# Sorting the edges of a graph layer on the chip into tile pairs, in place of fetching a row for each edge

## Chip, cores and metric

The kernel runs on 1 core of one Trainium2 chip. The metric is device microseconds for one execution. A core has TensorE (PE, matmuls), VectorE (DVE), ScalarE (ACT), GpSimd (POOL) and SyncE (SP), each of which executes its own instructions in program order and waits on semaphores for the others.

## The reference, cut to what matters

A small graph transformer of two layers over 625 nodes with 256 channels and 20000 edges (`src`, `dst`). The change lies in the first graph layer:

```
xl = (x @ W_l).reshape(625, 4, 64)
xr = (x @ W_r).reshape(625, 4, 64)
e = xl[src] + xr[dst]                      # 20000 x 256
e = where(e >= 0, e, 0.2 * e)
score = einsum('ehd,hd->eh', e, att)       # 20000 x 4
# softmax over the edges of each dst, then the weighted sum of xl[src] per dst
```

Beside it stand a token mixer on the same nodes (layer norm, a small attention, an MLP of 1024 hidden channels), then a mixture of 16 experts, then a second layer of the same kinds. Neither kernel differs in these.

## The kernel before

The softmax is done densely. Four scores for each edge are written to a table in HBM with a cell for each (dst, src) pair, of 625 x 625 cells, and a count of how often each pair occurs (`cnt`) is kept in SBUF; attention then runs over dense rows, with the logarithm of the count added. So the edge stage has two products, the scores in `pair_scores` and the counts in `cnt`, and it ends when the last score has landed: SP then loads the tables (L2282), and nothing of the rest can start before.

An edge column is 125 edges, one to a partition; there are 160 columns, in 32 groups of G = 5. For each group:

- GpSimd gathers the xl rows of a column with an indirect DMA (L2143) and scatters the four scores of an earlier column with another (L2153). There are two score tables, taken in turn, and a scatter waits until the one before it on the same table has landed. From group LATE = 12 on, two of five columns get their xl rows from TensorE instead and are not gathered.
- ScalarE makes the one-hot columns that select rows (`hot_rows`, L1888 and L1892).
- TensorE sums rows by multiplying the one-hots with all five node tiles, each in a high and a low part (`rows_of`, L544), and counts the pairs by multiplying two one-hot matrices (`count`, L522).
- VectorE adds gathered and computed rows (L1035, L1125), applies the leaky step (L1013), weighs by `att` (L1018), sums each head (L1021), and makes the one-hots of the counting (L1070, L1071).

The token mixer's steps are written in between the first groups by hand (L477 and L506 up to the MLP, L558 and L566). All groups from 16 to 31 stand in hardware loops.

## Time and profile before

| | |
|---|---|
| three runs | 1161.45, 1166.17, 1166.57 us (median 1166.17) |
| profiled execution, first to last instruction (span) | 1154.3 us |
| busy: PE, DVE, ACT, POOL | 948.9, 858.0, 466.5, 463.7 us |
| last scatter of the edge stage lands | 518.4 us |
| indirect DMAs in the edge stage | 160 scatters, 120 gathers |

The time of a run is the span and some 7 to 12 us around it. Differences are taken within the span and then set against the median. The stages follow each other: edges and mixer up to 518 us, dense attention, experts from about 620 us, the second layer, experts again to the end.

### The profile page before, as it was taken

To read this page: it belongs to the slowest core of one execution; us is meant where nothing else is said; L and a number is where in the kernel's file an instruction comes from. 1 tells how busy PE (TensorE), PEld (TensorE's weight loads), DVE (VectorE), ACT (ScalarE), POOL (GpSimd) and SP (SyncE) were. 2 spreads that over 40 slices of the span, in tenths; PEclk is the share of its full clock that TensorE was granted. 3 is DMA by queue.
4 is the path that set the end of the run, shared out by engine and by line. 5 is a ranking of instruction groups with operands and counts; after the bars stand their busy time and mean duration, and the time that the engine had idled before them with its cause. 6 is when DMAs were issued, how large, how long until landed. Compare 5 with 4: busy or idle time off the path is not lost.

```text
span 1154.3 us, 19240 instructions
## 1 busy us (share of the span) xinstructions
PE 948.9 (82%) x6532; PEld 829.5 (72%) x6532; DVE 858.0 (74%) x1953; ACT 466.5 (40%) x795; POOL 463.7 (40%) x374
## 2 busy tenths in 40 slices
PE   4586998879989998983835999985898588599996
PEld 2566886768978887853734999974588377589885
DVE  5659468869777978997987888776688765866635
ACT  1453755467858686616621111110253053212120
POOL 2448888877777877860001222250000000211104
PEclk9888999789999999997865999997999698699999
DMA  8962222323222232209704999983000000588883
GB/s 295 276 194 64 56 69 68 74 48 73 63 62 62 63 77 47 48 11 247 189 1 137 324 316 333 316 299 116 0 1 1 1 1 1 211 307 304 297 317 91
DMA packets 57946, 157.58 MB, mean 137 GB/s; under 512 B 23797, under 2 KB 32938, under 8 KB 49618
## 3 DMA queue, kind: packets, MB, share of 16 engines
q1 hardware_dynamic: 26830, 125.59, 33.3%
q0 software_dynamic: 25056, 24.10, 9.3%
q10 hardware_dynamic: 5992, 7.04, 1.7%
q8 instruction: 37, 0.61, 0.2%
q14 instruction: 31, 0.25, 0.1%
HBM read 136.50 MB, written 19.86 MB: 135 GB/s over the span
## 4 chain that ended last, share of the span: by engine, by line
PE 33%; DMA 24%; DVE 17%; POOL 12%; issue 10%; SPq 3%; POOLq 0%; ACT 0%; DVEq 0%; ACTq 0%
DMA pair_scores<-sc_ring,idx_ring 13%; PE bank L775 11%; PE bank L786 6%; POOL pair_scores L2153 5%; POOL arena L2143 5%; DMA arena<-pair_scores 4%; PE bank L544 3%; PE bank L708 2%; POOL arena L2208 2%; PE bank L496 2%; SPq L2232 2%; DMA arena<-slot_y,sloti 2%; DMA arena<-in_exp 1%; PE bank L697 1%; PE bank L874 1%
## 5 line engine op out<-in xcount | busy, mean ns | idle before, releaser
L2198 POOL DMA_INDIRECT arena<-row_tab,ids x42 | 57.7, 1373 | 493.7 <-DVE ids L1563 486.6
L2153 POOL DMA_INDIRECT pair_scores<-sc_ring,idx_ring x160 | 210.2, 1314 | 60.3 <-issue 43.4
L2143 POOL DMA_INDIRECT arena<-xl_tab,idx_ring x120 | 157.6, 1313 | 81.3 <-issue 31.7
L775 PE MATMUL bank<-arena 128*128 128x128 f32 x1480 | 180.8, 280 | 3.2 <-DMA arena<-in_exp 3.0
L775 PEld LDWEIGHTS bank<-arena 128*128 128x128 f32 x1480 | 175.0, 197 | 5.3 <-DMA arena<-in_exp 4.1
L1888 ACT ACTIVATE arena<-fmaps,node_neg 125x875 f32<-125x875 int32 x100 | 100.1, 1022 | 34.5 <-PE bank L544 34.5
L786 PE MATMUL bank<-arena 128*128 128x256 f32 (+1 forms) x404 | 97.6, 384 | 1.2 <-DMA arena<-in_exp0o 1.2
L1892 ACT ACTIVATE late_ohT<-arena 125x875 fp32r<-125x875 f32 x100 | 90.6, 926 | 0.0
L2021 ACT ACTIVATE arena<-bank 128x512 f32<-128x512 f32 (+2 forms) x76 | 34.4, 453 | 126.6 <-PE bank L775 126.5
L544 PE MATMUL bank<-late_hi,late_ohT 125*125 125x256 f32 x500 | 83.7, 298 | 0.6 <-DVE arena L1035 0.6
L786 PEld LDWEIGHTS bank<-arena 128*128 128x128 f32 (+1 forms) x404 | 72.1, 190 | 14.9 <-issue 6.0
L522 PE MATMUL bank<-tab 125*128 125x314 bf16 x400 | 62.3, 307 | 17.8 <-DVE tab L1071 17.8
L544 PE MATMUL bank<-late_lo,late_ohT 125*125 125x256 f32 x500 | 76.4, 283 | 0.0
L522 PE MATMUL bank<-tde 125*128 125x314 bf16 x400 | 62.0, 306 | 13.1 <-DVE tde L1071 13.0
L544 PEld LDWEIGHTS bank<-late_hi,late_ohT 125*125 125x125 f32 x500 | 68.8, 191 | 3.3 <-issue 0.9
L544 PEld LDWEIGHTS bank<-late_lo,late_ohT 125*125 125x125 f32 x500 | 67.2, 189 | 0.0
L1950 ACT ACTIVATE arena<-arena,rneg 125x625 f32<-125x625 f32 (+4 forms) x60 | 44.9, 748 | 52.5 <-DVE rneg L1361 26.9
L697 PE MATMUL bank<-ident,arena 125*125 125x125 f32 x260 | 44.1, 302 | 26.5 <-ACT arena L1950 25.5
L544 PE MATMUL bank<-late_hi,early_ohT 125*125 125x256 f32 x300 | 53.0, 312 | 15.4 <-DVE arena L1035 7.7
L1576 DVE TENSOR_TENSOR arena<-bank,arena 128x512 f32<-128x512 f32 (+2 forms) x76 | 37.2, 508 | 35.9 <-ACT arena L2021 35.9
L2000 ACT ACTIVATE arena<-bank 128x256 f32<-128x256 f32 x42 | 16.1, 383 | 116.1 <-DVE arena L1607 81.2
L522 PEld LDWEIGHTS bank<-tab 125*128 125x128 bf16 x400 | 37.2, 100 | 34.5 <-DVE tab L1071 14.9
(357 smaller groups left out, 2017.4 us busy)
## 6 DMA issues: line engine op xcount, KB each, us to landing
arena<-in_exp SPq DMA_DIRECT2D x25, 1024.0 KB, 7.1
arena<-in_exp SPq DMA_DIRECT2D x17, 1386.0 KB, 6.1
arena<-in_exp0o SPq DMA_DIRECT2D x25, 512.0 KB, 7.3
pair_scores<-cnt SPq DMA_DIRECT2D x10, 1093.8 KB
arena<-in_exp1o SPq DMA_DIRECT2D x17, 640.0 KB
fmaps<-in_rows SPq DMA_DIRECT2D x20, 437.5 KB, 3.8
arena<-pair_scores SPq DMA_DIRECT2D x7, 1093.8 KB
slot_y<-arena ACTq DMA_DIRECT2D x34, 128.0 KB, 6.4
```

Source lines behind the costliest of these rows:

```text
L522: mm = pe.matmul(banks[m][:, 0:CW], oh_dst[s][:, j, m * P:m * P + 128], oh_src[s][:, j, :], start=start and j == 0, stop=True, skip_group_ ...
L544: mm = pe.matmul(banks[T + r][0:P, i * D:(i + 1) * D], hot[late, s][:, t, at * P:(at + 1) * P], part[:, t, :], start=(n == 0 and t == 0), ...
L697: mm = pe.transpose(bank[0:P, t * P - off:t * P - off + P], prob[:, i % 3, t * P:(t + 1) * P], ident[0:P, 0:P])
L775: mm = pe.matmul(banks[1 + 2 * q + buf][0:rows, i * SLOTS:(i + 1) * SLOTS], w_in(s, q, k, m, rows), xsT[:, s, k, :], start=(k == 0), stop= ...
L786: mm = pe.matmul(banks[5 + s][:, 0:D], hid[0:rows, s, m, :], w_out(s, m), start=(m == 0), stop=(m == len(flat) - 1))
L1576: ins = v.tensor_tensor(hid[0:rows, s, m0:m0 + n, :], banks[(3 if rows == 128 else 1) + buf][0:rows, i0 * SLOTS:(i0 + n) * SLOTS] .rearran ...
L1888: a.activation(apart[late, s][:, t, :], edge_row[late, s][0:P, :], ACT.Abs, bias=node_neg[:, t:t + 1]).then_inc(sem("apart"), 1)
L1892: ins = a.activation(hot[late, s][:, t - 1, :], apart[late, s][:, t - 1, :], ACT.Relu, scale=-1.0, bias=1.0)
L1950: a.activation(prob[:, i % 3, 0:w], masked[:, i % 3, 0:w], ACT.Exp, bias=rneg[:, i:i + 1], scale=-1.0, accum_out=rden[:, i:i + 1]).then_in ...
L2143: p.indirect_dma_start(out=gat[:, b % 2, 0, j * D:(j + 1) * D], out_offset=None, in_=xl_tab, in_offset=bass.IndirectOffsetOnAxis(ap=idx_ri ...
L2153: p.indirect_dma_start(out=pair_scores[which], in_=sc_ring[:, b % 2, j, :], in_offset=None, out_offset=bass.IndirectOffsetOnAxis(ap=idx_ri ...
L2198: p.indirect_dma_start(out=xs[:, q, :], out_offset=None, in_=tab, in_offset=bass.IndirectOffsetOnAxis(ap=ids[:, q, :], axis=0))\
```

## The change

The edges are first sorted on the chip. A node tile is 125 nodes, so a (dst tile, src tile) pair is one of 25 buckets. VectorE marks the bucket of every edge (`find_buckets`), TensorE counts and ranks the edges in each, and every edge is given a slot, so that each column of 125 slots holds edges of one bucket only, with the rest of the bucket's last column empty. There are SORTED = 184 columns for the 160 of before. The sort itself is a product of one-hot matrices (`sort_edges`): for each of the 160 columns VectorE makes two 125x125 matrices (`choose_places`), GpSimd (three of four) or ScalarE (one of four) a 125x184 one (`find_column`, `find_columns`), and TensorE multiplies them.

Then the 184 columns go in 92 pairs. For a column one tile of xr and one of xl are enough: TensorE transposes two 125x125 one-hots, multiplies them for the counts (`turn_hots`), and sums rows with four matmuls whose second operand stands at an address taken from a register (`sum_rows`). ScalarE copies the one-hots and takes 0.4|z| of the rows (`copy_hots`, `read_rows`), the other part of the leaky step, 0.6z weighed by `att`, comes as four more channels of the tables (ROW = 260). VectorE makes the one-hots, adds the counts at a register address, weighs and sums (`make_hots`, `add_counts`, `score`). GpSimd only scatters; empty slots go to 125 spare cells. No xl table, no gather and no loads of edge rows are left. The mixer's steps stand at fixed pair numbers (`MIX`). All is written out, without loops.

```diff
+BUCKETS = T * T
+SORTED = (E + BUCKETS * (P - 1)) // P
+PAIRS = SORTED // 2
+assert SORTED % 2 == 0
 ROUNDER = 1.5 * 2 ** 23
+TAKEN = 3
+CHOSEN = 6
+HOTS = 3
+SCORED = 16
+MIX_BANKS = 3
...
+MIX = {"ln1": 6, "mixh": 8, "turned": 10, "xm": 11, "qkv_in": 12, "softened": 14, "turned_kq": 15, "kv": 17, "qkv": 18,
+       "attn": 20, "ln2": 22, "h2": 23, "h2T": 25, "m1": 26, "m2": 35, "added": 40}
...
+            def slots():
+                for i, b in enumerate(range(0, BUCKETS, 3)):
+                    after(pe, sem("slots_read"), i - 1)
+                    for q in range(b, min(b + 3, BUCKETS)):
+                        to = banks[3 + i % 2][0:P, (q - b) * EC:(q - b + 1) * EC]
+                        pe.matmul(to, before[:, :], member[:, q, :], start=True, stop=False)
+                        mm = pe.matmul(to, orders[:, q * P:(q + 1) * P], slots_before, start=False, stop=True)
+                    mm.then_inc(sem("slots"), 1)
...
+            def sort_edges():
+                for j in range(EC):
+                    pe.wait_ge(sem("chosen"), j + 1)
+                    if j % 4 == 3:
+                        pe.wait_ge(sem("act_columns"), j // 4 + 1)
+                    else:
+                        pe.wait_ge(sem("pool_columns"), j // 4 * 3 + j % 4 + 1)
+                    for w in range(2):
+                        mm = pe.matmul(banks[5 + w][0:P, 0:SORTED], chosen[:, j % CHOSEN, w, :],
+                                       columns16[:, j % CHOSEN, :], start=(j == 0), stop=(j == EC - 1))
+                    mm.then_inc(sem("placed"), 1)
...
+            def turn_hots(c):
+                pe.wait_ge(sem("onehot"), c + 1)
+                after(pe, sem("counted"), c - 1)
+                bank = banks[4 + c % 2]
+                to_d, to_s = (onehot[:, c // 2 % TAKEN, c % 2, w, :] for w in range(2))
+                pe.matmul(bank[0:P, 0:P], to_d, ident16[:, :], start=True, stop=True)
+                pe.matmul(bank[0:P, P:2 * P], to_s, ident16[:, :], start=True, stop=True)
+                pe.matmul(bank[0:P, 2 * P:3 * P], to_d, to_s, start=True, stop=True).then_inc(sem("turned_hots"), 1)
+            def sum_rows(i):
+                _, rows = nc.values_load_multi_w_load_instructions(
+                    at_rows[0:1, 2 * i:2 * i + 2, :].rearrange("p c w -> p (c w)"), engines=[mybir.EngineType.PE],
+                    min_val=0, max_val=(2 * T - 1) * ROW)
+                for c in range(2):
+                    pe.wait_ge(sem("hot"), 2 * i + c + 1)
+                    after(pe, sem("z_read"), 2 * i + c - 2)
+                    n = 0
+                    for w in range(2):
+                        for part in (hi_rows, lo_rows):
+                            mm = pe.matmul(banks[SUM_BANKS[(2 * i + c) % 3]][0:P, 0:ROW], hot[0:P, i % HOTS, c, w, :],
+                                           part[:, bass.ds(rows[2 * c + w], ROW)], start=(n == 0), stop=(n == 3))
+                            n += 1
+                    mm.then_inc(sem("z_made"), 1)
...
-            def late_group(g, b, segment):
-                s = b % 2
-                for r in range(NP):
-                    rows_of(g, s, 1, r)
-                    if r == 0:
-                        pe.wait_ge(sem("onehot"), g + (1 - BEHIND))
-                        if b == 0:
-                            pe.wait_ge(sem("counts_read"), segment)
-                    mm = count(s, COUNTED[r], b == 0)
...
+            sum_members()
+            pe.wait_ge(sem("ident"), 2)
+            sum_columns()
+            begin_blocks()
+            owners()
+            ring["n"] = 3
+            pe.wait_ge(sem("xn"), T)
+            to_fm("xnT0", xn)
+            slots()
+            pe.wait_ge(sem("wlr_in"), 16)
+            read_out(pe, "xnT0")
+            linear_tm("lr", fa, lambda k: W("lr", k), 2 * D)
+            sort_edges()
+            read_out(pe, "lr")
...
+            turn_hots(0)
+            turn_hots(1)
+            for i in range(PAIRS):
+                for c in (2 * i + 2, 2 * i + 3):
+                    if c < SORTED:
+                        turn_hots(c)
+                sum_rows(i)
+                mix(i)
...
+            def find_buckets():
+                dve.wait_ge(sem("edges_in"), 32 * len(PARTS))
+                own.link(v.tensor_copy(nodes_f, edge_ids[:, :, :]))
+                own.link(v.tensor_scalar(digits, nodes_f, float(P), None, ALU.is_ge))
+                for k in range(2, T):
+                    own.link(v.scalar_tensor_tensor(digits, nodes_f, float(k * P), digits, ALU.is_ge, ALU.add))
+                own.note(v.scalar_tensor_tensor(local, digits, -float(P), nodes_f, ALU.mult, ALU.add))
+                own.link(v.scalar_tensor_tensor(bucket, digits[:, 1, :], float(T), digits[:, 0, :], ALU.mult, ALU.add))
+                for b in range(BUCKETS):
+                    ins = v.tensor_scalar(member[:, b, :], bucket, float(b), None, ALU.is_equal)
+                ins.then_inc(sem("sorting"), 1)
+                own.link(v.tensor_scalar(local, local, 1.0, None, ALU.add))
...
+            def find_slots():
+                for i, b in enumerate(range(0, BUCKETS, 3)):
+                    n = min(3, BUCKETS - b)
+                    dve.wait_ge(sem("slots"), i + 1)
+                    v.tensor_tensor(slot_parts[:, b:b + n, :],
+                                    banks[3 + i % 2][0:P, 0:n * EC].rearrange("p (b j) -> p b j", b=n),
+                                    member[:, b:b + n, :], ALU.mult).then_inc(sem("slots_read"), 1)
+                dve.wait_ge(sem("slots_read"), (BUCKETS + 2) // 3)
+                own.link(v.tensor_reduce(slot_of, slot_parts.rearrange("p b j -> p j b"), AX.X, ALU.add))
+                rounded_of(column_of, slot_of, 1.0 / P, -float(P // 2) / P)
+                own.note(v.tensor_scalar(column_neg, column_of, -1.0, None, ALU.mult))
+                own.link(v.scalar_tensor_tensor(place_of, column_of, -float(P), slot_of, ALU.mult, ALU.add))
+                dve.sem_inc(sem("sorting"), 1)
...
+            def choose_places():
+                for j in range(EC):
+                    after(dve, sem("placed"), j - CHOSEN + 1)
                     for w in range(2):
+                        ins = v.tensor_scalar(chosen[:, j % CHOSEN, w, :], iota_c[:, 0:P], place_of[:, j:j + 1],
+                                              local[:, 1 - w, j:j + 1], ALU.is_equal, ALU.mult)
+                    ins.then_inc(sem("chosen"), 1)
...
+            def make_hots(i):
+                after(dve, sem("turned_hots"), 2 * (i - TAKEN + 1))
+                for c in range(2):
+                    for w in range(2):
+                        ins = v.tensor_scalar(onehot[:, i % TAKEN, c, w, :], iota_1[:, :],
+                                              node_at[:, w, 2 * i + c:2 * i + c + 1], None, ALU.is_equal)
+                    ins.then_inc(sem("onehot"), 1)
+            def add_counts(i):
+                if i == 0:
+                    dve.wait_ge(sem("cnt_zero"), 1)
+                if i % 4 == 0:
+                    n = min(8, SORTED - 2 * i)
+                    _, regs = nc.values_load_multi_w_load_instructions(
+                        at_counts[0:1, 2 * i:2 * i + n], engines=[mybir.EngineType.DVE], min_val=0, max_val=T * N - P)
+                    count_at[:] = regs
+                for c in (2 * i, 2 * i + 1):
+                    dve.wait_ge(sem("hot"), c + 1)
+                    after(dve, sem("counted"), c)
+                    to = cnt_flat[:, bass.ds(count_at[c % 8], P)]
+                    v.tensor_tensor(to, to, banks[4 + c % 2][0:P, 2 * P:3 * P], ALU.add).then_inc(sem("counted"), 1)
...
+            def score(i):
+                rows = weighed[:, i % 2, :, :, :]
+                dve.wait_ge(sem("z_read"), 2 * i + 2)
+                for c in range(2):
+                    ins = v.tensor_tensor(rows[:, c, :, 0:HD], rows[:, c, :, 0:HD],
+                                          Vt(0, "att").rearrange("p (h d) -> p h d", h=H), ALU.mult)
+                    own.note(ins)
...
+                    after(dve, sem(f"scattered{w}"), 16 * (i - SCORED + 1))
+                own.fence()
+                v.tensor_reduce(sc_ring[:, i % SCORED, :, :].rearrange("p c h -> p (c h)"),
+                                rows.rearrange("p c h d -> p (c h) d"), AX.X, ALU.add).then_inc(sem("scored"), 1)
...
+            split_rows()
+            read_nodes()
+            make_hots(0)
+            make_hots(1)
+            find_cells()
+            add_counts(0)
+            for i in range(PAIRS):
+                if i + 2 < PAIRS:
+                    make_hots(i + 2)
+                if i + 1 < PAIRS:
+                    add_counts(i + 1)
+                score(i)
+                mix(i)
+            dve.wait_ge(sem("counted"), SORTED)
...
-            def hot_rows(g, s, late):
-                act.wait_ge(sem(f"rows{s}"), g * 8 + (16 - 8 * s))
-                after(act, sem("z_made"), g * NP - NP)
-                for t in range(T + 1):
-                    if t < T:
-                        a.activation(apart[late, s][:, t, :], edge_row[late, s][0:P, :], ACT.Abs,
-                                     bias=node_neg[:, t:t + 1]).then_inc(sem("apart"), 1)
-                    if t > 0:
-                        act.wait_ge(sem("apart"), g * T + t)
-                        ins = a.activation(hot[late, s][:, t - 1, :], apart[late, s][:, t - 1, :], ACT.Relu,
...
+            def copy_hots(c):
+                act.wait_ge(sem("turned_hots"), c + 1)
+                after(act, sem("z_made"), 2 * (c // 2 - HOTS + 1))
+                a.activation(hot[0:P, c // 2 % HOTS, c % 2, :, :].rearrange("p w n -> p (w n)"),
+                             banks[4 + c % 2][0:P, 0:2 * P], ACT.Copy).then_inc(sem("hot"), 1)
+            def read_rows(i):
+                rows = weighed[:, i % 2, :, :, :]
+                after(act, sem("scored"), i - 1)
+                for c in range(2):
+                    act.wait_ge(sem("z_made"), 2 * i + c + 1)
+                    bank = banks[SUM_BANKS[(2 * i + c) % 3]]
+                    a.activation(rows[:, c, :, 0:HD], bank[0:P, 0:D].rearrange("p (h d) -> p h d", h=H), ACT.Abs, scale=0.4)
+                    a.activation(rows[:, c, :, HD], bank[0:P, D:ROW], ACT.Copy).then_inc(sem("z_read"), 1)
...
+            def find_column(j):
+                after(pool, sem("placed"), j - CHOSEN + 1)
+                p.tensor_scalar(columns16[:, j % CHOSEN, :], iota_c[:, :], column_of[:, j:j + 1], None, ALU.is_equal)\
+                    .then_inc(sem("pool_columns"), 1)
...
+            def scatter(c):
+                which, i = c % 2, c // 2
+                pool.wait_ge(sem("scored"), i + 1)
+                after(pool, sem(f"scattered{which}"), 16 * i)
                 p.indirect_dma_start(
+                    out=pair_scores[which], in_=sc_ring[:, i % SCORED, which, :], in_offset=None,
+                    out_offset=bass.IndirectOffsetOnAxis(ap=pair_cells[:, c:c + 1], axis=0))\```

What the engines execute in the stage, by the compiled programs. First TensorE, a stretch in the middle of a late group of before: `tab` is a counting one-hot, `late_ohT` the row-selecting one-hots, the rest are parts of the tables.

```order
L522 MATMUL bank<-tab 128x314 x10
L544 MATMUL bank<-late_hi,late_ohT 125x256 x5
L544 MATMUL bank<-late_lo,late_ohT 125x256 x5
L544 MATMUL bank<-late_xl_hi,late_ohT 125x256 x5
L544 MATMUL bank<-late_xl_lo,late_ohT 125x256 x5
```

And TensorE in the changed kernel, from the second column's one-hots of a pair to its first two row sums:

```order
L570 MATMUL bank<-ident,mask_words 125x125
L571 MATMUL bank<-ident,mask_words 125x125
L572 MATMUL bank<-mask_words 125x125
L576 TENSOR_LOAD at_rows
L576 ISA x8
L585 ISA
L585 MATMUL bank<-x_hi,hot 125x260
L585 REGISTER_ALU
L585 MATMUL bank<-x_lo,hot 125x260
```

Long runs of equal matmuls have become short ones, with a register load and its moves between them in every pair and a register instruction before each row sum.

VectorE, a stretch of a late group of before (`tde` is a counting one-hot, `tc` the rows to be scored):

```order
L1136 TENSOR_SCALAR arena<-bank 125x512
L1070 ISA
L1070 TENSOR_SCALAR tde<-iota_n,dstf 125x628
L1071 ISA
L1071 TENSOR_SCALAR tde<-iota_n,srcf,src_step 125x314
L165 ISA
L1139 TENSOR_TENSOR tc<-arena,bank 125x512
```

VectorE in the changed kernel, all of one pair (`mask_words` holds the one-hots, `tc` the rows):

```order
L1111 TENSOR_SCALAR mask_words<-iota,node_at 125x125 x4
L1128 ISA
L1128 TENSOR_TENSOR cnt<-cnt,bank 125x125
L1128 ISA
L1128 TENSOR_TENSOR cnt<-cnt,bank 125x125
L1137 TENSOR_TENSOR tc<-tc,vec 125x4x64 x2
L1143 TENSOR_REDUCE sc_ring<-tc 125x8
```

Nine instructions on 125 to 520 elements a partition take the place of ones on 256 to 1280; every fourth pair a load of eight registers comes before the counts.

GpSimd, from the end of its constants into the stage, before:

```order
L2132 IOTA iota_b 125x25
L2136 MEMSET block 32x32 x4
L2143 DMA arena<-xl_tab,idx_ring 125x256 x11
L2153 DMA pair_scores<-sc_ring,idx_ring 390625x4
L2143 DMA arena<-xl_tab,idx_ring 125x256
```

and in the changed kernel, through the stage to the experts' first gathers:

```order
L2106 MEMSET block 32x32 x4
L2113 TENSOR_SCALAR fmaps<-iota_c,tab 125x184 x120
L2132 MEMSET cnt 125x3125
L2120 DMA pair_scores<-sc_ring,pair_cells 390750x4 x184
L2145 DMA arena<-row_tab,ids 128x256 x4
```

The gathers are gone, 120 column operations stand ahead of the first scatter, and 184 scatters follow each other with nothing between.

## Rows read from the trace of the kernel before

**Rows 1.** Windows: length, busy of PE, PEld, DVE, ACT, POOL, clock, DMA share, GB/s.

```profile
400.00:450.00 50.00, 45.58 (x358) 41.07 (x358) 38.59 (x66) 36.38 (x41) 39.13 (x31) 0.97 0.27 66
500.00:520.00 20.00, 14.74 (x97) 9.55 (x96) 19.79 (x45) 4.76 (x7) 11.25 (x10) 0.91 0.09 7
```

**Rows 2.** Groups of GpSimd: x count | busy us, mean ns | idle before.

```profile
L2153 POOL DMA_INDIRECT pair_scores<-sc_ring,idx_ring x160 | 210.2, 1314 | 60.3 <-issue 43.4 <-DMA pair_scores<-sc_ring,idx_ring 16.9
```

**Rows 3.** Timeline of GpSimd, last scatters: start, us, what [idle before].

```profile
508.81 1.19 POOL L2153 DMA_INDIRECT pair_scores<-sc_ring,idx_ring  x1 [1.60 <-DMA pair_scores<-sc_ring,idx_ring]
510.31 1.24 POOL L2153 DMA_INDIRECT pair_scores<-sc_ring,idx_ring  x1 [0.30 <-issue]
512.31 1.25 POOL L2153 DMA_INDIRECT pair_scores<-sc_ring,idx_ring  x1 [0.77 <-issue]
```

**Rows 4.** The chain of waits at the stage's end: start, us, what.

```profile
515.86 2.54 DMA pair_scores<-sc_ring,idx_ring
...
520.16 11.73 DMA arena<-pair_scores
```

**Rows 5.** Timeline of VectorE at the start: first layer norm, from first to last.

```profile
5.71 1.73 DVE L966 BATCH_NORM_STATS2 stats<-x 125x6 f32<-125x256 f32 x5 [1.28 <-DMA x<-in_x]
...
10.38 1.70 DVE L973 TENSOR_SCALAR xn<-x,mv,rstd 125x256 f32<-125x256 f32 x5
```

**Rows 6.** Timeline of TensorE: first linear layer, and a linear layer of the mixer.

```profile
15.18 10.84 PE L496 MATMUL bank<-wres,fmaps 128*125 128x512 f32 x20 [0.64 <-DVE fmaps L989]
...
88.01 5.99 PE L496 MATMUL bank<-wres,fmaps 128*125 128x256 f32 x20 [2.81 <-DVE fmaps L1249]
```

**Rows 7.** Timeline of VectorE: small copies out of PSUM, back to back.

```profile
59.38 0.18 DVE L1204 COPY tde<-bank 125x32 f32<-125x32 f32 x1
59.47 0.41 DVE L1205 COPY tde<-bank 125x256 f32<-125x256 f32 x1
59.80 0.18 DVE L1204 COPY tde<-bank 125x32 f32<-125x32 f32 x1
```

**Rows 8.** Timeline of VectorE: one-hots, back to back, one and two pointer scalars.

```profile
164.40 0.38 DVE L1070 TENSOR_SCALAR tab<-iota_n,dstf 125x628 bf16<-125x628 f16 x1
164.70 0.36 DVE L1071 TENSOR_SCALAR tab<-iota_n,srcf,src_step 125x314 bf16<-125x314 f16 x1
164.97 0.62 DVE L1070 TENSOR_SCALAR tab<-iota_n,dstf 125x628 bf16<-125x628 f16 x1
```

**Rows 9.** Groups of VectorE by shape: the head sums.

```profile
L1021 DVE TENSOR_REDUCE sc_ring<-tc 125x20 f32<-125x1280 f32 x32 | 47.6, 1486 | 3.2 <-DVE tc L1018 1.4 <-DMA pair_scores<-sc_ring,idx_ring 1.1
```

**Rows 10.** Timeline of TensorE: row sums, five to a line, at either clock.

```profile
34.91 1.27 PE L544 MATMUL bank<-late_lo,early_ohT 125*125 125x256 f32 x5
35.98 1.27 PE L544 MATMUL bank<-late_hi,early_ohT 125*125 125x256 f32 x5
...
98.55 0.76 PE L544 MATMUL bank<-late_hi,early_ohT 125*125 125x256 f32 x5
99.14 0.76 PE L544 MATMUL bank<-late_lo,early_ohT 125*125 125x256 f32 x5
```

**Rows 11.** Timeline of SyncE: two issues with one register load between them.

```profile
632.80 0.34 SPq L2318 DMA_DIRECT2D arena<-in_exp  x1
633.90 0.34 SPq L2309 DMA_DIRECT2D arena<-in_exp0o  x1
```

**Rows 12.** Groups of TensorE by shape: the mixer's MLP, up to 640 us.

```profile
L566 PE MATMUL bank<-arena 128*125 128x256 f32 x80 | 17.8, 379 | 0.0
L558 PE MATMUL bank<-fmaps,wres 128*128 128x375 f32 x32 | 11.5, 480 | 2.4 <-DVE fmaps L989 2.4
L558 PE MATMUL bank<-fmaps,wres 128*128 128x250 f32 x32 | 8.0, 374 | 0.0
```

**Rows 13.** Timeline of TensorE: two more pieces of the mixer.

```profile
44.57 4.45 PE L506 MATMUL bank<-fmaps,wres 128*128 128x375 f32 x16 [0.95 <-DVE fmaps L989]
...
59.09 4.38 PE L589 MATMUL bank<-fmaps,mixk 128*32 128x375 f32 x8 [6.50 <-DVE tde L1205]
```

**Rows 14.** Windows again, short ones, for the granted clock (before the DMA share).

```profile
235.00:240.00 5.00, 2.16 (x19) 1.95 (x17) 4.83 (x6) 5.00 (x9) 4.09 (x4) 1.00 0.15 30
600.00:605.00 5.00, 0.55 (x3) 0.55 (x4) 4.52 (x24) 0.00 (x0) 0.00 (x0) 0.50 0.00 0
```

1015 lines of the change are left out of this document (410 added, 605 removed).

## The prediction, made before the result was known

> **What bounds the kernel now.** I read the windows first, then the groups of GpSimd, then the chain. In the middle of the edge stage no engine is idle for long [rows 1]: of 50 us TensorE is busy for 45.6, VectorE for 38.6, ScalarE for 36.4, GpSimd for 39.1. At the stage's end VectorE is (19.8 of 20). So there is no single wait that the change could remove. The reader should see that GpSimd has 160 scatters at 1.31 us each [rows 2], that two scatters on different tables are issued 1.5 us apart (510.31 after 508.81), and on one table 3.5 us apart (512.31 after 508.81) [rows 3], since the second must wait for a landing of 2.54 us. The chain says what the stage's end is worth [rows 4]: the last scatter is issued at 515.86 and lands at 518.40, then the tables are loaded (11.73 us from 520.16), and all that follows waits for that. After this point both kernels do the same. So the question is one number: when does the last of 184 scatters land, against 518.4. Every microsecond there is one in the time. The profiled span is 1154.3, some 12 us under the median of 1166.2; I add the difference to the median. The three runs lie 5 us apart, so under 0.5% (6 us) is no change.
>
> **Up to the first column.** Before the first scatter everything must now be sorted. The edges are there at about 5 us (x lands at 5.7 [rows 5]); the buckets are 25 one-hots of 160 elements and some ten operations on 160 to 320, 7 us, to 12. Then four hand-overs between VectorE and TensorE, each of some small operations and a semaphore either way: I take 3 us each (bounds 1.5 and 4.5), to 24. The layer norm, which now stands behind them, took 5.71 to 12.08, 6.4 us [rows 5], to 30. Transposes and slots: 50 matmuls of 160 columns, with nine products of 480 elements behind them, 14 us (10.5 to 19), to 44. The slots are summed by a reduction of 4000 elements and some more small operations, 7 us, to 51. TensorE's first linear layer took 10.84 us [rows 6] and stands before the sort's matmuls, to 62. Only six columns of one-hots (CHOSEN) can be made ahead of it.
>
> **The sort** runs at VectorE's pace. A small operation costs its elements and a fixed part: a copy of 32 elements takes 0.09 us from start to start, one of 256 takes 0.33 [rows 7], so 1.07 ns an element and 0.06 fixed. A one-hot of 628 elements with one pointer scalar takes 0.30 and one of 314 with two takes 0.27 [rows 8]; a quarter of the time per element fits both, with some 0.065 for each pointer. For 125 elements with two pointers that gives 0.22 at that rate and 0.32 at the copy's; I take 0.27, since the 314-element row has the very same form. Two of them and a wait are 0.57 us a column; 154 columns are 88 us, with a tail 90, to 152 (133 with the low ends throughout, 170 with the high ones). GpSimd has 2.3 us for its three 184-element columns out of four. No row shows such an operation; bounds are nothing (hidden under VectorE) and one indirect issue, 1.19 us [rows 3], which would make 0.89 us a column and 50 us more. I take it as hidden. Splitting the tables into high and low parts is three passes over 2560 elements at the copy's rate, 8.4 us, to 161.
>
> [...]
>
> **A pair of columns.** GpSimd: with one scatter per table and pair, the wait for the same table sets 3.5 us by [rows 3] and issue alone 3.0; I take 3.4. VectorE: four one-hots of one pointer, 0.8; two adds of counts at a register address, 125 elements out of PSUM, 0.3 each; two weighings of 256, 0.33 each and a little; a reduction of 520, by 1486 ns for 1280 [rows 9] 0.63; a share of the register load, 0.3: together 3.2. ScalarE: 1.4. TensorE: eight row sums and six matmuls of 125 columns. Five row sums on 256 columns took 1.07 us from start to start (34.91 to 35.98) and 0.59 (98.55 to 99.14) [rows 10], at the two clocks, so 0.118 or 0.214 each; with a register load of up to 0.76 us (632.80 to 633.90 less the issue, SyncE's, the only one to be seen) [rows 11] and register instructions, 2.4 or 3.7 us. So at full clock GpSimd, VectorE and TensorE stand at 3.4, 3.2 and 2.4: no engine is much ahead, and 92 pairs at 3.4 would be 313.
>
> **The mixer lies on top.** Its MLP takes TensorE 37.3 us [rows 12], its other parts some 27 (4.5 for the MLP-like product of 44.57 [rows 13], 6.0 for the attention's last [rows 6]), VectorE some 40. It stands at pairs 6 to 40 only. Pairs 0 to 5 and 41 to 91 are 57 at 3.4, 194 us. In pairs 6 to 25 VectorE has 20 times 3.2, 34 of the mixer, and waits for TensorE's pieces that stand behind row sums in program order: before, such a wait was 6.50 us ahead of the piece at 59.09 [rows 13]; I take 20 in all: 118. Queued behind each of them are the next pair's one-hots, for which TensorE and then GpSimd wait; a ring of 16 pairs of scores doesn't help, since GpSimd is never that far behind. Pairs 26 to 40: TensorE has 15 times 2.6 and 37 of the MLP, 76. With 5 for filling and the last landing the loop is 393.
>
> **Sum.** 161 + 393 = 554 against 518.4 [rows 4]: 35 us more. 1166 + 35 = 1201. What is removed (120 gathers, the five-tile row sums, the counting over 314 and 628 elements) needs no term of its own, since the stage is summed anew.
>
> **The rivals.**
> *Not paid back* (the forecast, 0.45): some 160 us of preparation, then 393. Its own range, from the bounds of the sort (−20, +18) and of the loop (−8, +15), is 1175 to 1230.
> *Small operations are cheap* (0.30), the other side. If a one-hot is 0.22 and the hand-overs 1.5 us each, blocks begin at 143 or before; if scatters then come every 3.2 us and half of the mixer's 77 us goes into VectorE's and TensorE's gaps, the loop is 294 + 55 + 5 = 354, and the stage ends at 490 to 505: 1138 to 1153. For it: the low ends are rows too, and no engine is full in a pair. Against it: VectorE is full in the mixer's pairs by my sum. It decides when the last scatter is issued before 510; with blocks from 143 that needs under 4.0 us per pair on average. [...]
> *TensorE at half clock* (0.16). [...] At half clock a pair is 3.7 us and the mixer 1.6 times as long: a loop of 450, the stage's end at 611 less what overlaps, some 605: 1250 to 1260. [...]
> *Register loads are dear* (0.09). If the load in every pair stops TensorE, or every fourth pair VectorE, for 1.5 us and more in place of 0.76 and 1.2, that is 0.3 to 0.7 us a pair, 30 to 60 in all: 1235.
>
> **How the numbers follow.** The likeliest case gives 1201. The range 1140 to 1265 runs from the low end of the cheap case to just past the half clock: outside lie the case below 1140 (0.05) and combinations of the dear ones with slow GpSimd columns (0.08). Faster by over 0.5%: 0.27, the cheap case less 0.03 that ends within 6 us of no change. Within: that and 0.04 of the forecast's case, 0.07. Slower: 0.41 + 0.16 + 0.09 = 0.66.
>
> **What would show it.** In the profile of the changed kernel: the first scatter at about 168 us, the one-hots of the sort 0.27 us apart in VectorE's timeline and each column 0.57; the windows from 350 on with a scatter every 1.7 us, both GpSimd and VectorE over 0.8 busy, and the granted clock near 1.00; in pairs 6 to 25 idle times of VectorE before the mixer's operations, with TensorE as releaser; the last landing near 554. Wrong at once: a first scatter before 145, or pairs that come at 3.0 us or under, for which two tables can't be what limits them; or above 4 us after the mixer has ended, which would point at TensorE's clock or the register loads.

## The result, and the profile after

The changed kernel takes 1264.74 us (median of four runs, 1261.63 to 1269.24), the kernel before 1164.11 on the same chip: 1.088 times as long, 95% interval 1.084 to 1.092. So it is 100.6 us slower, where I had forecast 35.

The profiled execution spans 1264.0 us, and its own time was 1265.78. In all runs on record the time is 1.7 to 2.1 us over the span. So the 7 to 12 us that I had put around the span of the kernel before are no fixed part: its profiled execution, at 1154.3, was one of its faster ones. The two profiles are 109.7 us apart for the 100.6 of the medians. The chain of waits shows where the edge stage ends; its columns are start, us, what.

```profile
611.46 2.99 DMA pair_scores<-sc_ring,pair_cells
...
615.31 2.75 DMA pair_scores<-sc_ring,pair_cells
...
618.92 3.26 DMA pair_scores<-sc_ring,pair_cells
...
623.46 12.67 DMA arena<-pair_scores
```

The last scatter lands at 618.92 + 3.26 = 622.2 us, against 518.4 [rows 4]: 104 us later, and I had said 554. What follows took 641.8 us, against 635.9. Before the first scatter, VectorE's timeline is this (start, us, what, in brackets the idle time before and who ended it):

```profile
24.11 1.71 DVE L985 BATCH_NORM_STATS2 stats<-x 125x6 f32<-125x256 f32 x5
...
36.22 0.66 DVE L1071 TENSOR_TENSOR arena<-bank,tde 125x480 f32<-125x480 f32 x1 [5.76 <-PE bank L548]
39.59 0.66 DVE L1071 TENSOR_TENSOR arena<-bank,tde 125x480 f32<-125x480 f32 x1 [2.71 <-PE bank L548]
...
61.74 6.84 DVE L1075 TENSOR_REDUCE tab<-arena 125x160 f32<-125x4000 f32 x1
...
82.47 85.82 DVE L1086 TENSOR_SCALAR mask_words<-iota_c,tab 125x125 bf16<-125x125 f16 x308 [8.15 <-PE bank L560]
```

The hand-overs end at 24 and the layer norm at 30.5, as worked out. Then the slots take until 61.7, not 44: VectorE is idle for 2.7 to 2.8 us before each product, and the releaser is TensorE's L548. The sort of 308 one-hots takes 85.8 us, 0.279 each, 0.56 a column. GpSimd's first scatter is issued at 192.8; I had said about 168.

In the pairs after the mixer, VectorE has this pattern, here for one group of four pairs:

```profile
481.55 0.27 DVE L1128 TENSOR_TENSOR cnt<-cnt,bank 125x125 f32 x1
482.02 0.28 DVE L1128 TENSOR_TENSOR cnt<-cnt,bank 125x125 f32 x1 [0.20 <-DVE cnt L1128]
484.05 0.76 DVE L1137 TENSOR_TENSOR tc<-tc,vec 125x256 f32<-125x256 f32 x2 [1.74 <-ACT tc L1879]
484.94 0.69 DVE L1143 TENSOR_REDUCE sc_ring<-tc 125x8 f32<-125x520 f32 x1
...
487.80 0.69 DVE L1143 TENSOR_REDUCE sc_ring<-tc 125x8 f32<-125x520 f32 x1
```

From head sum to head sum it is 2.9, 4.7, 4.8 and 4.6 us, again and again from pair 41 on: 4.24 on average (402.8 to 614.5 for 50 steps), where I had 3.4. TensorE's timeline in the same stretch:

```profile
486.80 0.22 PE L572 MATMUL bank<-mask_words 125*125 125x125 bf16 x1
487.15 0.24 PE L570 MATMUL bank<-ident,mask_words 125*125 125x125 bf16 x1
487.23 0.22 PE L571 MATMUL bank<-ident,mask_words 125*125 125x125 bf16 x1
487.28 0.22 PE L572 MATMUL bank<-mask_words 125*125 125x125 bf16 x1
488.92 0.58 PE L585 MATMUL bank<-x_hi,hot 125*125 x1 [1.42 <-ACT hot L1869]
489.30 0.42 PE L585 MATMUL bank<-x_lo,hot 125*125 x1
489.51 0.42 PE L585 MATMUL bank<-x_hi,hot 125*125 x1
489.73 0.42 PE L585 MATMUL bank<-x_lo,hot 125*125 x1
```

Row sums start 0.216 us apart, which is the pace at half clock (0.214 in [rows 10]; 0.12 at a clock of 1.00 in the kernel with eight more matmuls, below, 480.85 to 480.97), and 1.42 us of idle time stand before the first. The profile names ScalarE's copy as releaser, but that copy ended at 487.9 (0.86 us from 487.06). What else stands there in the program is the register load. Its records in the trace (engine's sequencer, operation, durations in ns, first and last start):

```profile
L576 PEldq FUSED_REGOPS  x368: 146/148/165, 186.4 to 610.5; - x184
L576 PEldq SEQ_ASSERT  x368: 18/18/24, 186.6 to 610.7; - x184
L576 PEldq TENSOR_LOAD <-at_rows x92: 327/332/518, 185.8 to 609.3; - x92
```

So in each of 92 pairs TensorE executes the load and eight more instructions, two for each of four values. In the pair shown they run from 487.17 to 488.66, just the time of the gap.

The waits of VectorE and TensorE over the whole span (us in total, times, longest) and the windows (columns as in [rows 1]):

```profile
DVE tc L1137 <- ACT tc L1879: 67.8, 47, 3.1
DVE cnt L1128 <- issue: 45.8, 23, 3.3
PE bank L570 <- DVE cnt L1128: 70.9, 36, 8.5
PE bank L585 <- ACT hot L1869: 58.2, 69, 1.5
```

```profile
100.00:150.00 50.00, 40.87 (x180) 25.85 (x178) 50.00 (x178) 15.46 (x45) 50.00 (x67) 0.50 0.00 1
550.00:600.00 50.00, 32.51 (x168) 28.48 (x168) 29.79 (x104) 18.70 (x72) 28.51 (x24) 0.60 0.07 3
```

No engine is busy for more than two thirds of the pairs' time, and the granted clock is 0.60. ([rows 14], read by TensorE's busy time alone, don't carry over: in the sort's window TensorE was busy for 40.87 of 50 us, and the clock was 0.50.) So both dear rivals have their sign in the profile: the half clock, and the register loads (23 waits of 2.0 us on VectorE with "issue" as the releaser are just its 23 loads). The experiments had to tell them apart.

### The profile page after: what moved, and what is told of

Same layout as the page of the kernel before. It is cut to its first block, busy times and chain, and to the rows that moved or that the text cites. A ratio compares the mean times of both kernels' runs of the same rounds, so it can differ in the third digit from the quotient of the medians.

```text
span 1264.0 us, 20533 instructions
## 1 busy us (share of the span) xinstructions
PE 922.7 (73%) x5479; PEld 772.5 (61%) x5479; DVE 863.3 (68%) x2569; ACT 350.7 (28%) x1061; POOL 419.1 (33%) x401
## 4 chain that ended last, share of the span: by engine, by line
PE 45%; DVE 28%; DMA 10%; issue 9%; DVEq 2%; ACT 2%; POOL 2%; SPq 0%; POOLq 0%; ACTq 0%
PE bank L794 10%; PE bank L585 7%; DVE mask_words L1086 7%; PE bank L805 5%; DMA arena<-pair_scores 3%; PE bank L727 3%; DMA arena<-in_exp 3%; DVEq L1121 2%; DVE tc L1137 2%; PE bank L490 2%; POOL arena L2155 2%; PE bank L570 2%; PE bank L548 2%; DVE mask_words L1111 2%; PE bank L603 1%
## 5 line engine op out<-in xcount | busy, mean ns | idle before, releaser
L2120 POOL DMA_INDIRECT pair_scores<-sc_ring,pair_cells x184 | 224.7, 1221 | 217.9 <-DVE sc_ring L1143 149.7
L2145 POOL DMA_INDIRECT arena<-row_tab,ids x42 | 57.4, 1368 | 502.4 <-DVE ids L1528 495.4
L585 PE MATMUL bank<-x_hi,hot 125*125 x368 | 148.3, 413 | 70.6 <-ACT hot L1869 58.2
L585 PEld LDWEIGHTS bank<-x_hi,hot 125*125 125x125 f32 x368 | 101.3, 275 | 84.3 <-issue 83.8
L585 PE MATMUL bank<-x_lo,hot 125*125 x368 | 133.6, 372 | 0.0
L2113 POOL TENSOR_SCALAR fmaps<-iota_c,tab 125x184 bf16<-125x184 f16 x120 | 96.1, 819 | 70.7 <-DVEq L1079 62.1
L1137 DVE TENSOR_TENSOR tc<-tc,vec 125x256 f32<-125x256 f32 x184 | 69.8, 421 | 68.1 <-ACT tc L1879 67.8
L1878 ACT ACTIVATE tc<-bank 125x256 f32<-125x256 f32 x184 | 70.5, 383 | 155.9 <-PE bank L585 137.7
L570 PE MATMUL bank<-ident,mask_words 125*125 125x125 bf16 x184 | 51.0, 283 | 76.5 <-DVE cnt L1128 70.9
L585 PEld LDWEIGHTS bank<-x_lo,hot 125*125 125x125 f32 x368 | 104.0, 283 | 0.0
L1869 ACT ACTIVATE hot<-bank 125x250 fp32r<-125x250 f32 x184 | 64.8, 380 | 117.6 <-PE bank L572 113.5
L1128 DVE TENSOR_TENSOR cnt<-cnt,bank 125x125 f32 x184 | 52.0, 282 | 66.5 <-issue 45.8
L1086 DVE TENSOR_SCALAR mask_words<-iota_c,tab 125x125 bf16<-125x125 f16 x320 | 89.1, 390 | 8.1 <-PE bank L560 8.1
L570 PEld LDWEIGHTS bank<-ident,mask_words 125*125 125x125 bf16 x184 | 32.5, 177 | 90.9 <-issue 65.9
L560 PE MATMUL bank<-fmaps,mask_words 125*125 125x184 bf16 x320 | 71.5, 361 | 22.3 <-POOL fmaps L2113 14.5
L560 PEld LDWEIGHTS bank<-fmaps,mask_words 125*125 125x125 bf16 x320 | 45.4, 205 | 48.8 <-DVE mask_words L1086 41.5
L716 PE MATMUL bank<-ident,arena 125*125 125x125 f32 x260 | 44.8, 306 | 39.5 <-ACT arena L1933 38.5
L1143 DVE TENSOR_REDUCE sc_ring<-tc 125x8 f32<-125x520 f32 x92 | 63.9, 695 | 10.6
## 6 DMA issues: line engine op xcount, KB each, us to landing
arena<-in_exp0o SPq DMA_DIRECT2D x25, 512.0 KB, 7.2
```

Source lines behind the costliest of these rows:

```text
L560: mm = pe.matmul(banks[5 + w][0:P, 0:SORTED], chosen[:, j % CHOSEN, w, :], columns16[:, j % CHOSEN, :], start=(j == 0), stop=(j == EC - 1))
L570: pe.matmul(bank[0:P, 0:P], to_d, ident16[:, :], start=True, stop=True)
L585: mm = pe.matmul(banks[SUM_BANKS[(2 * i + c) % 3]][0:P, 0:ROW], hot[0:P, i % HOTS, c, w, :], part[:, bass.ds(rows[2 * c + w], ROW)], start ...
L1086: ins = v.tensor_scalar(chosen[:, j % CHOSEN, w, :], iota_c[:, 0:P], place_of[:, j:j + 1], local[:, 1 - w, j:j + 1], ALU.is_equal, ALU.mult)
L1137: ins = v.tensor_tensor(rows[:, c, :, 0:HD], rows[:, c, :, 0:HD], Vt(0, "att").rearrange("p (h d) -> p h d", h=H), ALU.mult)
L1143: v.tensor_reduce(sc_ring[:, i % SCORED, :, :].rearrange("p c h -> p (c h)"), rows.rearrange("p c h d -> p (c h) d"), AX.X, ALU.add).then_ ...
```

## The experiments

**1. Without register loads, with loads ahead, with more matmuls.** Three kernels against one another. The first has constant addresses:

```diff
-                _, rows = nc.values_load_multi_w_load_instructions(
-                    at_rows[0:1, 2 * i:2 * i + 2, :].rearrange("p c w -> p (c w)"), engines=[mybir.EngineType.PE],
-                    min_val=0, max_val=(2 * T - 1) * ROW)
...
-                                           part[:, bass.ds(rows[2 * c + w], ROW)], start=(n == 0), stop=(n == 3))
+                                           part[:, w * ROW:(w + 1) * ROW], start=(n == 0), stop=(n == 3))
...
-                    to = cnt_flat[:, bass.ds(count_at[c % 8], P)]
+                    to = cnt_flat[:, c % 8 * P:c % 8 * P + P]
```

> The kernel after the change, but with no register loads in the pairs: TensorE's row sums read tile 0 for every column and VectorE adds all counts to the first 1000 columns of the count table, so scores and counts are wrong values; number and sizes of instructions stay. In the changed kernel four late pairs take 2.9, 4.7, 4.8 and 4.6 us. Theory A (register loads stop the engines): about 1.3 us of TensorE's idle time before row sums and 2 us of VectorE's before every fourth pair's counts vanish, the late pairs come at 3.4 us or less, the last scatter lands 60 to 80 us earlier and the time is near 1190. Theory B (half clock): the chain of one-hots, transposes, copies and row sums at half clock sets the pace; the pairs gain under 0.5 us, the time stays over 1225.

Measured: 1187.01 us, 78 less, as theory A had it. Late pairs come every 2.83 us, the last head sum starts at 500.3 in place of 614.5.

> The same computation as the changed kernel, with each register load written earlier: TensorE's before the transposes of the next pair, VectorE's before the wait of the score in the pair before. If a load costs because it stands behind a wait and its latency is then open (theory A), most of what the kernel without loads gains is kept: 30 to 60 us less than 1265. If what costs is the issue of the load and its moves, which stay, under 15 us. Theory B (half clock): under 10 us.

```diff
...
             for i in range(PAIRS):
+                rows = load_rows(i)
                 for c in (2 * i + 2, 2 * i + 3):
                     if c < SORTED:
                         turn_hots(c)
-                sum_rows(i)
+                sum_rows(i, rows)
...
```

Measured: 1219.62, 45 less. TensorE no longer waits before its row sums, and the pairs take 2.8, 3.1, 3.1 and 5.6 us. The 5.6 stands where VectorE loads, after its counts:

```profile
491.54 0.28 DVE L1127 TENSOR_TENSOR cnt<-cnt,bank 125x125 f32 x1 [0.20 <-DVE cnt L1127]
494.77 0.76 DVE L1143 TENSOR_TENSOR tc<-tc,vec 125x256 f32<-125x256 f32 x2 [2.95 <-ACT tc L1888]
```

ScalarE's result that is named here was there at 494.06; the load is what was late.

> The changed kernel with eight more 125-column matmuls in each pair, four before each wait for a column's copied one-hots, into a bank that is overwritten after; the result is the same. Theory B (the half clock makes the row sums slow): the granted clock of the late pairs rises from 0.57 to 0.64 to near 1.0, the eight row sums of a pair take 1.0 us in place of 1.9, and the time falls by 20 to 60 us although work was added. Theory A: the clock may rise, but the pace stays at 4.2 us or gets worse by the 0.4 to 0.8 us of the added matmuls, as far as they don't fit in the waits: 1265 to 1310.

```diff
                 for c in range(2):
+                    after(pe, sem("z_read"), 2 * i + c - 2)
+                    for _ in range(4):
+                        pe.matmul(banks[SUM_BANKS[(2 * i + c) % 3]][0:P, 0:P], ident16[:, :], ident16[:, :],
+                                  start=True, stop=True)
                     pe.wait_ge(sem("hot"), 2 * i + c + 1)
-                    after(pe, sem("z_read"), 2 * i + c - 2)
```

Measured: 1271.0, 6 more, with runs that overlap (1268.67 to 1274.98). In the window from 450 to 500 us the clock was 0.83, for 0.60 in the changed kernel, but the pairs came no faster (4.35 on average, for 4.24). The window of the kernel with loads ahead says the same from the other side:

```profile
450.00:500.00 50.00, 30.63 (x255) 27.82 (x256) 29.85 (x104) 17.74 (x68) 28.25 (x24) 0.83 0.07 3
```

```profile
450.00:500.00 50.00, 32.80 (x184) 29.00 (x183) 35.99 (x125) 21.11 (x79) 32.13 (x28) 0.64 0.08 3
```

The first is the kernel with eight matmuls more, at 4.35 us a pair, the second the one with loads ahead, at 0.64 of the clock and 3.7 us a pair. So the half clock was there, and it doesn't set the pace: a clock of 0.83 brought nothing, and at 0.64 the pairs were faster. The added matmuls take time of their own (four of them 0.20 us from their start to the row sum behind, 480.33 to 480.53, and 0.38 at half clock, 489.80 to 490.18), so the kernel with eight more can't exclude a small gain by itself; the kernels without checks, below, put a price on the clock.

**2. What in a load costs.** The program has, behind every load, two instructions for each value that check its bounds (the part on the change took the eight at L576 for moves). VectorE's, by the compiled order:

```
L1121 TENSOR_LOAD at_counts
L1121 ISA x16
```

In the changed kernel's trace such a load takes 0.60 us and the two checks of a value 0.18 and 0.02.

They can be left out where a value can't be out of bounds (here it comes from a table of 25 made on the chip). First with the loads ahead, then in place on both engines, then in place on TensorE alone:

```diff
...
                     at_rows[0:1, 2 * i:2 * i + 2, :].rearrange("p c w -> p (c w)"), engines=[mybir.EngineType.PE],
-                    min_val=0, max_val=(2 * T - 1) * ROW)
+                    min_val=0, max_val=(2 * T - 1) * ROW,
+                    skip_runtime_bounds_check_because="a tile number made on the chip from a table of 25")
...
```

> As the kernel with the register loads ahead, and each loaded value goes into its register without the instructions that check its bounds; the same computation. That kernel's late pairs take 2.8, 3.1, 3.1 and 5.6 us: the fourth holds VectorE's load of eight registers with its 16 instructions, 2.95 us of idle time. If the loads' instructions are what costs there (about 0.1 us each), the 5.6 becomes 4.3 or less and the time falls 15 to 30 us, to 1190 to 1205. If it is the load's own latency, the 5.6 stays and so do the 1220.

Measured: 1193.90 us.

> The changed kernel with its register loads where they were, and only the instructions that check the bounds of the loaded values left out (two for each value: 8 in every pair on TensorE, 16 in every fourth pair on VectorE); the same computation. If the checks were nearly all of the loads' cost, most of the 71 us that the kernel with both edits gained over the changed one is here too: 1195 to 1210. If the place counted as much on TensorE (its idle 1.3 us before row sums), 1215 to 1235.

Measured: 1194.60 us. In its trace L576 has 92 loads of 0.33 us and none of the 736 other instructions.

> As the kernel with bare loads in place, but only TensorE's loads are without the instructions that check bounds; VectorE's keep their 16. The same computation. It divides the 70 us of the checks between the engines: by TensorE's idle time before its row sums (58 us) and VectorE's before its counts (46 us) in the changed kernel's chain of waits both count; VectorE's is 2 to 3 us in each of 23 loads. If the parts add up, VectorE's checks keep some 25 to 40 us: 1220 to 1235. If TensorE's checks alone were the pace, about 1200.

Measured: 1210.74 us, less than the 1220 to 1235 expected. Without checks the place doesn't matter (1193.9 and 1194.6 have overlapping runs). Of the 70 us of time, TensorE's checks are 54 and VectorE's the last 16. But that isn't how long each held up the scores:

| kernel | last head sum starts | last scatter issued | time |
|---|---|---|---|
| changed | 614.5 | 618.9 | 1264.7 |
| TensorE's checks out | 556.0 | 570.3 | 1210.7 |
| both engines' checks out, in place | 512.9 | 554.0 | 1194.6 |
| no loads | 500.3 | 546.4 | 1187.0 |
| no loads, four tables | 503.0 | 512.0 | 1155.0 |

TensorE's checks held up the last scores by 58.5 us and VectorE's by 43.1, more than the 25 to 40 that I had put for them. Only 16 of the 43 show in the time, since the scatters stay behind: the last one is issued 4 us after the last head sum in the changed kernel and 41 us after it without checks. Part 3 is on that wait. Pairs with VectorE's checks alone take 2.8 to 3.5 us, and every fourth 4.6 on average. In the kernel with bare loads ahead there are stretches at half clock, with TensorE no less on time:

```profile
483.86 0.42 PE L589 MATMUL bank<-x_lo,hot 125*125 x1
484.23 0.34 PE L570 MATMUL bank<-ident,mask_words 125*125 125x125 bf16 x1
...
485.02 0.56 PE L589 MATMUL bank<-x_hi,hot 125*125 x1
485.38 0.42 PE L589 MATMUL bank<-x_lo,hot 125*125 x1
485.60 0.42 PE L589 MATMUL bank<-x_hi,hot 125*125 x1
```

From the second on the row sums are still 0.216 us apart, and the gap of 1.42 us before them is gone. From head sum to head sum a pair takes 2.8 to 3.5 us. In this kernel's trace the 13 late pairs at a mean clock of 0.50 take 3.09 us on average, the 17 at 1.00 take 2.96; with the loads in place 12 take 3.21 and 24 take 2.85 (without the last of all). So a pair at half clock is 0.1 to 0.4 us longer, and the checks cost 1.3 (4.24 to 2.97 with the loads in place).

**3. What holds it then.** The kernel without loads gives its last scores at 500, but its last scatter is issued at 546.4.

> The kernel without register loads (row sums read tile 0, counts go to the first 1000 columns), with the scatters taken in turn to four tables, of which only two are read later, so that half the scores are left out as well. Without loads VectorE gives scores every 2.85 us a pair, yet the scatters come every 3.8 us a pair and the last one is issued at 546.5, 46 us after the last scores. If the wait for the scatter before on the same table is what holds GpSimd, pairs of scatters now come at 3.0 us, the last one is issued before 510, and the time is near 1145, under the kernel before. If the scatters are slow by themselves, 1180 to 1190.

```diff
-                after(pool, sem(f"scattered{which}"), 16 * i)
+                after(pool, sem(f"scattered{c % 4}"), 16 * (c // 4))
                 p.indirect_dma_start(
-                    out=pair_scores[which], in_=sc_ring[:, i % SCORED, which, :], in_offset=None,
+                    out=pair_scores[c % 4], in_=sc_ring[:, i % SCORED, which, :], in_offset=None,
```

Measured: 1154.97 us, last scatter issued at 512.0, the pairs of scatters 2.98 us apart; I had expected before 510 and near 1145. First GpSimd's timeline of the kernel without loads, on two tables, then the scatters of the one with four (durations in ns, first and last start):

```profile
542.27 1.19 POOL L2112 DMA_INDIRECT pair_scores<-sc_ring,pair_cells  x1 [0.94 <-DMA pair_scores<-sc_ring,pair_cells]
544.07 1.18 POOL L2112 DMA_INDIRECT pair_scores<-sc_ring,pair_cells  x1 [0.60 <-issue]
546.45 1.19 POOL L2112 DMA_INDIRECT pair_scores<-sc_ring,pair_cells  x1 [1.19 <-DMA pair_scores<-sc_ring,pair_cells]
```

```profile
L2113 POOL DMA_INDIRECT pair_scores<-sc_ring,pair_cells x184: 1182/1187/2162, 188.4 to 512.0; - x184
```

And GpSimd's timeline of the one with four, at the end:

```profile
488.06 1.19 POOL L2113 DMA_INDIRECT pair_scores<-sc_ring,pair_cells  x1 [0.30 <-issue]
489.55 1.19 POOL L2113 DMA_INDIRECT pair_scores<-sc_ring,pair_cells  x1 [0.30 <-issue]
```

On two tables a table's next scatter comes 4.2 us after the last (542.27 to 546.45), on the late stretch 3.8 on average: more than the 3.5 of [rows 3]. In the chain of the kernel without loads the last landings take 2.75 to 3.31 us with 0.86 us from each to the next issue on its table; in [rows 4] a landing took 2.54. That wait was hidden in the changed kernel, whose scores came every 4.24 us, and became the bound as soon as the checks were gone. It kept back 32 us (1187 to 1155). With four tables the scatters are 1.49 us apart, GpSimd's 1.19 for an issue and 0.30 between two. So the next bound, its issuing, stands at 2.98 us a pair. And the landings, mostly 2.6 us up to 490, grow to 6.04 for the very last, issued at 512.01; why isn't shown. The kernel with four tables leaves half of the scores unread, so it is a measurement and no version to use.

**4. The start.**

> The same computation, with the start shortened at two places: the 25 matmul pairs of the slots use two bf16 halves in place of one fp32 operand (29 us from 32.7 to 61.7 in the changed kernel, where I had put 14), and VectorE copies the transposed nodes before the slots and not behind their reduction, so that the first linear layer lies beside the reduction of 6.8 us. If the start is in series with all the rest, the first scatter comes 25 us earlier than 192.8 and the time falls by as much, to 1240. If the rest has slack (the mixer's weights, the blank tables), under 10 us.

```diff
-                        mm = pe.matmul(to, orders[:, q * P:(q + 1) * P], slots_before, start=False, stop=True)
+                        pe.matmul(to, orders16[:, q * P:(q + 1) * P], slots_hi, start=False, stop=False)
+                        mm = pe.matmul(to, orders16[:, q * P:(q + 1) * P], slots_lo, start=False, stop=True)
...
+            from_fm("xnT0", fa)
             find_slots()
...
-            from_fm("xnT0", fa)
```

Measured: 1248.24, 16.5 less, where I had expected 25. Three buckets take 2.33 us in place of 3.44; the halves' preparation costs 3 us. The first scatter comes 13.2 us earlier and the last 12.5: the start is in series with the rest, but I had put too much on it. The other 4 or so of the 16.5 us lie behind the edge stage, which the edit doesn't touch.

> The changed kernel, with ScalarE making two of four 184-element columns of the sort and GpSimd two, for one and three; the same computation. In the changed kernel 160 sort columns take 92 us, 0.57 each, with both VectorE (two one-hots of 0.29) and GpSimd (three of four columns at 0.76) busy all the time. If GpSimd's columns set the pace, a column takes under 0.5 us now and the first scatter comes 10 us or more earlier than 192.8. If VectorE's one-hots do, the pace stays within 0.02 us of 0.57 and the first scatter within 3 us.

Here the edit is `j % 2` for `j % 4` where columns are dealt out. Measured in one run, which alone says little of the time: 1258.97. The one-hots come 0.267 us apart (294 in 78.4 us) in place of 0.279, the first head sum 3.2 us earlier. A column is thus 0.53 us, a little outside the 0.02 that I had allowed if VectorE sets the pace, and far from the pace under 0.5 if GpSimd did.

> As the kernel with ScalarE making half of the columns, and VectorE's one-hots of the sort without the multiplication by the node's number, so with one pointer scalar and not two; all edges then count as node 1 of their tiles, scores and counts are wrong, and only the sort's stretch is to be read. If the second pointer scalar costs its 0.065 us as I had worked out, a one-hot takes 0.22 us and a column 0.45; if the price of a short one-hot is a fixed one, it stays at 0.28 and 0.57.

```diff
-                                              local[:, 1 - w, j:j + 1], ALU.is_equal, ALU.mult)
+                                              None, ALU.is_equal)
```

```profile
89.86 52.74 DVE L1086 TENSOR_SCALAR mask_words<-iota_c,tab 125x125 bf16<-125x125 f16 x286 [0.36 <-PE bank L560]
```

286 one-hots in 52.7 us are 0.184 each, 0.37 a column. So with GpSimd relieved VectorE sets the sort's pace, and the second pointer scalar costs 0.08 of the 0.267. (Its time as a whole, 3264 us, says nothing of the sort: all edges now have node 1 of their tile, and the scatters write one cell over and over.)

**5. All together.**

> The same computation with all edits that helped one by one: loads ahead and without checks (1193.9), the short start (16.5 us less than the changed kernel), ScalarE making half of the sort's columns (3 to 6 us). If the stages are in series these add up: 1172 to 1176, still some 10 us over the kernel before. The scatters, 3.75 us a pair on two tables, are then what sets the end after the mixer, with the last scatter issued near 532.

Measured: 1176.88 us (1167.54 to 1179.92), ratio to the kernel before 1.011 (1.007 to 1.016). The stages add up to within 1 us of what was expected.

> As the kernel with all repairs, with the mixer's steps spread over pairs 6 to 78 in place of 6 to 40. While the mixer's steps stand between the pairs GpSimd waits for scores, and after them it falls behind by 37 us. If the end is set by GpSimd's scatters, an even spread lets them run nearly through from the first one: 92 pairs at 3.75 are 345 us, the last scatter is issued near 515 to 520 and the time is 1157 to 1163, the kernel before's. If the mixer's steps cost the same wherever they stand, or hold up GpSimd in both places, 1170 to 1176.

```diff
-MIX = {"ln1": 6, "mixh": 8, "turned": 10, "xm": 11, "qkv_in": 12, "softened": 14, "turned_kq": 15, "kv": 17, "qkv": 18,
-       "attn": 20, "ln2": 22, "h2": 23, "h2T": 25, "m1": 26, "m2": 35, "added": 40}
+MIX = {"ln1": 6, "mixh": 9, "turned": 12, "xm": 15, "qkv_in": 18, "softened": 22, "turned_kq": 25, "kv": 28, "qkv": 31,
+       "attn": 35, "ln2": 40, "h2": 44, "h2T": 48, "m1": 50, "m2": 70, "added": 78}
```

```profile
L2142 POOL DMA_INDIRECT pair_scores<-sc_ring,pair_cells x184: 1183/1188/1795, 165.9 to 519.7; - x184
```

Measured: 1165.66 us, 11.2 less than with the mixer in pairs 6 to 40; ratio to the kernel before 1.002 (0.999 to 1.004), so no difference from it is shown, and 3 us over the expected 1157 to 1163. The last scatter is issued at 519.7 in place of 535.3. It is still behind the last head sum by 26 us: the scatters' wait on two tables remains the bound.

## Why the prediction was wrong in size

The direction and the main mechanism were right (a start of some 160 us is not paid back), the size was not: 101 us and not 35. By its own steps, in the profile:

- **Up to the slots**: right. 24 for the hand-overs and 30.5 for the layer norm against 24 and 30.
- **Transposes and slots, 14 us**: wrong, 31 (30.5 to 61.7). The term took 50 matmuls of 160 columns alike, 0.28 us each. The 25 with an fp32 operand take 0.82, and 1.15 with the bf16 one ahead. With the bf16 halves a bucket takes 0.78.
- **The sort, 0.57 a column and 90 us**: right, 0.56. That VectorE sets it holds too, but GpSimd's columns were hidden only just: in the sort's window both engines were busy for 50.00 of 50 us. With fewer of GpSimd's columns VectorE's one-hots came 0.01 us faster each; why isn't shown.
- **First scatter at 168**: 192.8, 25 late, of which the slots are 17. The other 8 lie between the sort's end (168.3, for 152) and the first scatter. The first pair's register loads are in them: without loads the first head sum starts 5.6 us earlier (185.5 for 191.1).
- **A pair at 3.4 us**: wrong, and this is the step that failed most. VectorE's own prices held: 2.83 us a pair without loads, against 3.2 less 0.3 for the load, and one-hots, counts, weighings and the head sum stand in the trace near what I took (from start to start 0.65 us for four one-hots; 0.28 for a count, 0.76 for two weighings, 0.69 for the head sum; taken: 0.8, 0.3, 0.33 for each of two and a little, 0.63). What failed is the register loads. I took TensorE's as up to 0.76 us, from SyncE's row [rows 11], and counted it as work beside others. It is 1.5 us with its checks (487.17 to 488.66), and it stood in the path of one-hots, row sums and scores. A share of 0.3 us for VectorE's was 0.5 (45.8 us of waits in 92 pairs) to 0.7 (2.6 to 2.95 every fourth pair, with loads ahead). That the loads carry two checks a value was to be read in the compiled order, which the part on the change even shows (eight of them in a pair on TensorE), and they were given no price. They cost 70 us of time and 102 us at the last scores; the result lies 64 us above the forecast.
- **The rival of dear loads** (0.09, 30 to 60 us) had the cause, and its condition was met: a load with its checks takes 1.5 us on TensorE, and VectorE waited for 2.0 us at each of its loads. Its size was low and it got too small a chance.
- **The rival of the half clock** (0.16, 1250 to 1260) came nearest in time by the wrong way. The clock was indeed 0.53 to 0.60 in the windows of the late pairs. And yet pairs at 0.50 took 3.1 to 3.2 us once the checks were gone. My 3.7 us a pair added up TensorE's work as if it were the bound.
- **Scatters at 3.4 us a pair**: a bound that I put too low, hidden in the changed kernel and seen without the checks: 3.8. The rival of cheap operations, with its 3.2 a pair, would have failed on it; its sum was wrong besides, since half of 77 us is 38.5 and it added 55.
- **The mixer**: pairs 0 to 40 took 212 us (head sums, 191.1 to 402.8), and I had 214. That is luck, two errors that cancel: without loads the same stretch takes 173 us, so the loads cost 39 there, and the mixer was hidden by about so much more than I had put. The 50 steps after it took 212 us, where 3.4 each makes 170, and the last scatter landed 7.7 us after the last head sum had started, for the 5 that I had put.
- **The case below 1140** (0.05): no run shows a one-hot that costs hardly more than the 0.09 us of the 32-element copy [rows 7]. One of 125 elements took 0.279 in the sort, 0.267 with GpSimd relieved and 0.184 with one pointer scalar.
- **After the edge stage** I had assumed no difference. It took 5.9 us more in the profile. In the profiles of eleven variants of the changed kernel (all but the one with one pointer) it is 635 to 638, so the change in itself doesn't lengthen it. Set against the kernel with the short start, some 3 of the 5 us come in between 740 and 820 us, in the experts; the cause stays open.

What stays open: the cheapest way past the scatters' wait. Two more tables would have to be loaded and merged, and that wasn't tried. Nor was a sort with some of its one-hots on ScalarE.

## What to carry to other kernels

Count every instruction that the compiled order shows, the ones that only touch registers too, and ask on which side of a wait they stand: a load of a value into a register costs little by itself (leaving out all 115 of them gained 8 us more here, 1194.6 to 1187.0), and two checks for each value cost 70 us. When no engine is full and a lower clock and idle gaps are seen together, take away one of them before explaining with either: extra matmuls raised the clock from 0.60 to 0.83 and brought nothing. When two causes are taken away in turn, look at the stage's own product and not only at the time: VectorE's checks seemed worth 16 us and held up the scores by 43, since the scatters had become the bound. When one wait is mended, look at once for the next one on the engine that only issues: the scatters needed 3.8 us a pair on two tables whenever scores were ready, and spreading other work evenly beside them was worth 11 us.

## What was not expected of the hardware

- Instructions that check the bounds of loaded values: VectorE's load of eight values with 16 of them left it idle for 2.0 us at a time in the changed kernel (45.8 us in 23 waits) and for 2.6 to 2.95 in the late pairs of the kernel with loads ahead. Without them a pair with a load is 0.4 us longer than the others in the kernel with bare loads ahead, and no longer in the one with bare loads in place. TensorE's 8 in each pair made up to 1.5 us of idle time before the row sums.
- A VectorE one-hot of 125 elements took 0.184 us with one pointer scalar and 0.267 with two.
- 184 scatters whose rows go to very few cells took from 166 to 2620 us, 13.4 us from one to the next on average (1.5 to 31), while the issue on GpSimd stayed at 1.19 us. Why they are slow isn't shown.
- The landing of a scatter isn't one price. The 2.54 us of [rows 4] was a short one of the kernel before, whose chain also has 2.78, 3.02 and 4.01. At the end of the changed kernel's stage it was 2.75 to 3.26, and with four tables 6.04 for the last.
